# Two layers of gated recurrence and feed-forward on one core: first batch in channel halves, paired reciprocals, sums on GpSimd, idle-time products on TensorE, and a new order

## The chip, the core and the metric

The kernel runs on one core of a Trainium2 chip. The core's engines work side by side and wait for each other through semaphores: TensorE (PE, matmuls; PEld is its weight load), VectorE (DVE), ScalarE (ACT), GpSimd (POOL) and SyncE (SP, here only DMA issues). The metric is the device time of one execution in microseconds. All data is float32 but for two small bfloat16 masks.

## The reference

Four batches b of 256 tokens with 256 channels pass two layers l. Each layer has a conditioning part and a feed-forward part. The conditioning part is the same in both, with parameters w and u of its own (k and v are one input, `fside_BxSxS_0`; r is x):

```python
tf = sigmoid(sum(time_emb))
decay = exp(-exp(w)) * (0.5 + 0.5 * tf)
ek = exp(min(k, 30));  ekv = ek * v
# over tokens, forward and backward: a = a * decay + ekv ; b = b * decay + ek
num = nf + nb - ekv + exp(min(u + k, 30)) * v
den = df + db - ek + exp(min(u + k, 30))
out = sigmoid(r) * (num / max(den, 1e-8)) * (0.8 + 0.2 * tf)
```

Layer 0's feed-forward part adds to x a shared gated MLP (width 704) and eight routed experts (width 176, two per token, 320 slots each; a token's slot is its rank among the tokens of that expert in order). Layer 1's adds `relu(h @ W_up) @ W_down`, and `h @ W_expert` scaled by the weights of the two best of eight gates.

## The kernel before

**Tiles.** A tile n = 4 l + b is the conditioning part of one layer and batch, 128 partitions by 2 channel halves (c = 0, 1) by 256 tokens. `euk` (exp(u + k)) becomes the denominator and then its reciprocal; `euv` is euk * k and becomes the numerator; `df` and `nf` hold the scans of ek and ekv; `xc` holds x by channels and becomes h, the input of the feed-forward part.

**DVE** is the engine of the recurrence. `wkv(l, b, step)` has six steps: 0 forward scans of ek into df (L597, two, one per half); 1 forward scans of ekv into nf, and the cap on the next batch's ek (L609); 2 backward scans of df (L604), whose input `gd` ScalarE has scaled (L445); 3 euk + df (L639) and the floor at 1e-8 (L640); 4 backward scans of nf, and the cap on the next euk (L613); 5 two reciprocals (L647). For tiles 0 and 3 DVE then makes h too (L650, L653, L656); for tiles 1 and 2 GpSimd does (L343, L348, L351). In layer 1 step 5 ends with L660.

**The shared MLP** of a batch is six chunks c: TensorE multiplies h by up to 256 weight columns into one of three PSUM banks hb (`shared_up`), ScalarE takes the silu of one half (`silu`, L492), DVE multiplies by the other (`hidden`, L684). A bank is free when its chunk's `hidden` is done. `shared_down` closes a batch. `turn_rows` transposes h and makes the router's logits.

**Order.** Every engine's program is written out by tables indexed by the chunk c. `STEPS0` and `STEPS1` say how many steps of tiles 1 to 3 and 4 to 7 DVE does ahead of `hidden(c)`; `TURN_AT`, `RANK_AT`, `DOWN_BEHIND` place TensorE's transposes, ranks and down products; `ROUTE_AT` and `PLACE_AT` place DVE's routing of three rounds (batches 0 and 1; 2; 3); `SPREAD` places GpSimd's scatters of token rows to the experts' slots in DRAM (L355, two DMAs per 128 tokens). Tile 0's six steps come before everything else.

**After the last scatter** SP loads the slots (`buf`, L290, L291), TensorE transposes them and runs the eight experts (chunks 19 to 34), and DVE fits layer 1's tiles between. Then come batch 3's last shared chunks, 16 gathers of expert rows by GpSimd (L403; into the room of ek for batches 0 and 1 and of ekv for 2 and 3), and layer 1's feed-forward, batch after batch.

## Time and profile before

| | us |
|---|---|
| median of 3 runs (178.6 to 180.64) | 179.05 |
| the profiled execution's own time | 179.44 |
| its span, first to last instruction | 177.7 |
| PE busy, of the span | 144.6 |
| DVE busy | 134.6 |
| ACT busy | 71.2 |
| POOL busy | 69.2 |

A busy share is an average over stages with different limits, so the place of an idle stretch counts for more than its size. A timeline row gives start, length, engine, line, operation and tiles; "[x <-y]" is the engine's idle time just ahead of it and what ended it. One matmul of the program is two records of the trace.

### The profile page before, as it was taken

The page shows a single profiled execution, that of the slowest core. Times are in us where ns is not written, and L with a number is a line of the kernel's source. Part 1 is how long each engine was busy: PE and PEld are TensorE (multiplying, and loading weights), DVE is VectorE, ACT ScalarE, POOL GpSimd, SP SyncE. Part 2 cuts the span into 40 slices and gives each one's busy share as a digit, 9 for nine tenths or more (in the row PEclk, how much of TensorE's full clock was granted, in tenths as well). Part 3 has the DMA queues.
Part 4 walks back from the last instruction along what each step waited for, and adds up shares of the span by engine and source line. Part 5 has one row for each costly group of instructions (what it writes and reads, how often), then busy time and mean ns, then how long its engine had stood idle before and what let it go on. Part 6 is the DMA issues. An engine that isn't in the chain of part 4 may idle for free.

```text
span 177.7 us, 2207 instructions
## 1 busy us (share of the span) xinstructions
PE 144.6 (81%) x666; PEld 117.6 (66%) x666; DVE 134.6 (76%) x293; ACT 71.2 (40%) x168; POOL 69.2 (39%) x83
## 2 busy tenths in 40 slices
PE   0000297799999969995999999899999977999992
PEld 0000285688898858883777877677788856878781
DVE  0899979999998996724499969967589434787624
ACT  3699374454053005223427534623633201232330
POOL 5388022732487770560050050050002577762130
PEclk9999999789999999999999999999999999999998
DMA  4999999995002320129702072012104033332111
GB/s 96 255 340 369 395 413 258 194 279 200 1 31 96 111 87 32 37 48 331 281 1 74 3 221 74 30 44 76 61 17 148 30 116 90 112 101 89 59 59 59
DMA packets 14843, 23.61 MB, mean 133 GB/s; under 512 B 1974, under 2 KB 10375, under 8 KB 14704
## 3 DMA queue, kind: packets, MB, share of 16 engines
q1 hardware_dynamic: 13296, 19.49, 35.1%
q0 software_dynamic: 1536, 3.99, 7.1%
q8 instruction: 5, 0.08, 0.2%
q14 instruction: 6, 0.05, 0.1%
HBM read 15.29 MB, written 8.39 MB: 133 GB/s over the span
## 4 chain that ended last, share of the span: by engine, by line
PE 40%; DVE 33%; issue 9%; DMA 7%; POOL 7%; ACT 2%; SPq 0%; DVEq 0%; POOLq 0%; ACTq 0%
PE hb L833 23%; PE dn L833 10%; DVE euk L647 9%; POOL ek L403 4%; DVE df L604 4%; DVE nf L604 3%; PE tp L847 3%; DVE euk L639 2%; DMA buf<-slots_in 2%; DMA ekv<-slots_out,get_at 2%; DMA cond_s<-cond 2%; POOL ekv L403 2%; PE tp L923 2%; PE dk L833 2%; DVE df L597 1%
## 5 line engine op out<-in xcount | busy, mean ns | idle before, releaser
L833 PE MATMUL hb<-xc,sup_s 128*128 128x256 f32 x176 | 43.1, 404 | 2.3 <-DVE hid L684 2.3
L833 PEld LDWEIGHTS hb<-xc,sup_s 128*128 128x128 f32 x176 | 35.3, 204 | 8.2 <-DVE hid L684 3.1
L492 ACT ACTIVATE gate_a<-hb 128x256 f32<-128x256 f32 (+3 forms) x40 | 16.1, 403 | 35.5 <-PE hb L833 28.3
L343 POOL TENSOR_TENSOR euv<-euv,nf 128x512 f32<-128x512 f32 x6 | 7.8, 1296 | 55.6 <-DVE nf L604 55.6
L833 PE MATMUL hb<-bufT,mup_s 128*112 128x320 f32 (+1 forms) x96 | 27.3, 434 | 1.0 <-issue 0.5
L647 DVE RECIPROCAL euk<-euk 128x256 f32<-128x256 f32 x16 | 26.8, 1714 | 0.0
L847 PE MATMUL tp<-turn,xc 128*128 128x136 f32 x32 | 5.5, 325 | 22.4 <-DVE xc L656 22.4
L833 PEld LDWEIGHTS hb<-bufT,mup_s 128*112 128x112 f32 (+1 forms) x96 | 17.1, 181 | 9.1 <-issue 1.7
L833 PE MATMUL dn<-mdn_s,hidm 112*128 112x256 f32 x96 | 22.1, 380 | 0.0
L833 PE MATMUL dn<-sdn_s,hid 128*128 128x256 f32 x96 | 21.7, 381 | 0.1
L355 POOL DMA_INDIRECT slots_in<-htok,put_at x16 | 16.3, 1019 | 10.2 <-DVE put_at L729 5.8
L847 PEld LDWEIGHTS tp<-turn,xc 128*128 128x128 f32 x32 | 5.0, 225 | 22.9 <-issue 20.9
L833 PEld LDWEIGHTS dn<-sdn_s,hid 128*128 128x128 f32 x96 | 18.0, 190 | 2.8 <-DVE hid L684 0.5
L833 PEld LDWEIGHTS dn<-mdn_s,hidm 112*128 112x128 f32 x96 | 17.8, 190 | 2.7 <-issue 0.3
L684 DVE TENSOR_TENSOR hidm<-hb,gate_a 112x320 f32<-112x320 f32 (+1 forms) x16 | 7.6, 483 | 11.1 <-ACT gate_a L492 11.0
L684 DVE TENSOR_TENSOR hid<-hb,gate_a 128x256 f32<-128x256 f32 (+1 forms) x24 | 9.5, 412 | 4.6 <-ACT gate_a L492 4.5
L604 DVE TENSOR_TENSOR_SCAN df<-dk,df,gd 128x255 f32<-128x255 f32 x16 | 11.0, 724 | 0.9 <-ACT gd L445 0.9
L604 DVE TENSOR_TENSOR_SCAN nf<-dk,nf,gn 128x255 f32<-128x255 f32 x16 | 11.0, 731 | 0.1
L337 POOL TENSOR_TENSOR euv<-euk,k 128x512 f32<-128x512 f32 x8 | 10.2, 1274 | 0.4 <-DVE euk L613 0.4
L597 DVE TENSOR_TENSOR_SCAN df<-dk,ek 128x256 f32<-128x256 f32 x16 | 10.1, 668 | 0.0
L597 DVE TENSOR_TENSOR_SCAN nf<-dk,ekv 128x256 f32<-128x256 f32 x16 | 10.0, 661 | 0.0
L403 POOL DMA_INDIRECT ek<-slots_out,get_at x8 | 7.7, 956 | 5.6 <-DVE euk L660 3.5
(107 smaller groups left out, 203.1 us busy)
## 6 DMA issues: line engine op xcount, KB each, us to landing
mup_s<-mup SPq DMA_DIRECT2D x4, 704.0 KB, 15.3
slots_in<-outb SPq DMA_DIRECT2D x10, 256.0 KB, 9.2
slots_out<-outb SPq DMA_DIRECT2D x8, 256.0 KB, 2.2
...
```

Of the source, the lines that this page charges most:

```text
L337: nc.gpsimd.tensor_tensor(euv[:, n % 2], euk[:, l, b], k[:, b], ALU.mult).then_inc(euv_ready, 1)
L343: nc.gpsimd.tensor_tensor(euv[:, n % 2], euv[:, n % 2], nf[:], ALU.add).then_inc(num_ready[n], 1)
L355: nc.gpsimd.indirect_dma_start(out=slots_in, out_offset=bass.IndirectOffsetOnAxis(ap=put_at[:, j, n:n + 1], axis=0), in_=htok[:, n], in_of ...
L403: nc.gpsimd.indirect_dma_start(out=got_of(b, j, i), out_offset=None, in_=slots_out, in_offset=bass.IndirectOffsetOnAxis(ap=get_at[:, j, b ...
L492: nc.scalar.activation(dst, src, ACT.Silu).then_inc(silu_ready, 1)
L597: nc.vector.tensor_tensor_scan(fwd[:, c], d, src[:, b, c], 0.0, ALU.mult, ALU.add).then_inc(fwd_done, 1)
L604: nc.vector.tensor_tensor_scan(rev(both[:, c, 0:T - 1]), d, rev(gained[:, c, 0:T - 1]), both[:, c, T - 1:T], ALU.mult, ALU.add).then_inc(b ...
L639: after(tick(nc.vector.tensor_tensor(eu, eu, df[:], ALU.add)))
L647: nc.vector.reciprocal(eu[:, c], eu[:, c]).then_inc(den_ready, 1)
L684: nc.vector.tensor_tensor(dst, up, g, ALU.mult).then_inc(hid_ready, 1)
L833: return nc.tensor.matmul(dst, w, m, start=first, stop=last)
L847: last = nc.tensor.matmul(tp[i][:, at:at + P + E], xc[:, b, c, i * P:(i + 1) * P], turn[:, c], start=c == 0, stop=c == CH - 1, skip_group_ ...
```

## The change

- **First batch in halves.** Tile 0 is done by `first_tile` on DVE and `first_half` on GpSimd: both backward scans, the floor, the reciprocal and the product for half 0, then the same for half 1. `first_products` on TensorE does the transposes and the first four chunks (AHEAD) for half 0 when that half of h is there, and accumulates half 1 onto it. Those four chunks use three hb banks and one dn bank.
- **Paired reciprocals.** Tiles 1 to 7 form `pair` = d0 * d1 of the two halves, one reciprocal of 256 columns, and `rden` = pair times the denominators with halves exchanged.
- **Sums on GpSimd.** euk + df (`denominator`), the floor (for tiles not in MAX_ON_VECTOR), the numerator, and numerator times gated x run on GpSimd. The product with rden stays on DVE but for tile 1.
- **Idle-time products.** `idle_products` multiplies ident by k into a dn bank that nobody reads: 8 after the second forward scan of tile 0, 14 ahead of the transposes of batch 1.
- **Small ones.** The load of wu_s is issued by ScalarE; tf comes from a tanh; the router one-hots take fewer instructions; the output scale of layer 1 moves from L660 into ScalarE's relu and the mixing weights; the silu table is loaded by a dummy call; the gathers of batches 0 and 1 go into `buf` and wait for the stores and the transposes, not for the last tile; the memsets of padding move behind batch 1's work.
- **New order.** All tables have new numbers.

```diff
-TURN_AT = (6, 9, 14)
-ROUTE_AT = (6, 9, 14)
-RANK_AT = (8, 11, 15)
-PLACE_AT = (7, 10, 14)
-FETCH_AT = 23
+EARLY_AT = 2
+EARLY = 8
+FILL = {3: 14}
+AHEAD = 4
+
+TURN_AT = (3, 10, 15)
+ROUTE_AT = (3, 10, 15)
+RANK_AT = (6, 11, 15)
+PLACE_AT = (4, 12, 15)
+FETCH_AT = 28
...
-STEPS0 = (6, 0, 0, 3, 1, 0, 1, 1, 0, 2, 2, 1, 1, 0, 0, 0, 0, 0, 0)
-STEPS1 = (0, 0, 0, 0, 0, 0, 0, 0, 0, 0, 0, 0, 0, 0, 1, 0, 0, 2, 0, 1, 1, 1, 0, 3, 0, 2, 1, 4, 1, 0, 0, 1, 0, 2, 0)
-DOWN_BEHIND = (8, 13, 18)
-TAKE_BEHIND = (10, 16, 17)
-GATE_AT = (0, 5)
-SPREAD = {0: 1, 1: 4, 10: 5, 11: 5, 14: 5, 15: 8}
-H0_ON_VECTOR = (0, 3)
+STEPS0 = (4, 4, 0, 1, 0, 1, 1, 0, 1, 1, 1, 2, 0, 2, 0, 0, 0, 0, 0)
+STEPS1 = (0, 0, 0, 0, 0, 0, 0, 0, 0, 0, 0, 0, 0, 0, 0, 0, 0, 0, 5, 0, 0, 2, 2, 0, 0, 3, 0, 0, 1, 3, 0, 2, 0, 2, 0)
+DOWN_BEHIND = (7, 13, 17)
+TAKE_BEHIND = (13, 16, 18)
+GATE_AT = (3, 10)
+SPREAD = {7: 0, 9: 2, 10: 3, 14: 6, 15: 8}
+H0_ON_VECTOR = (0, 2, 3)
+Q1_ON_VECTOR = (0, 1, 2, 3)
+PADS_AT = (5, 5, 5, 5, 5, 5)
+MAX_ON_VECTOR = (1, 3, 4)
...
-        got = ek[:].rearrange("p b c t -> p (b c t)").rearrange("p (k n d) -> p k n d", k=2, n=TB * 2)
+        got = buf[:].rearrange("p q r d -> p (q r) d")[:, 0:8].rearrange("p (k n) d -> p k n d", k=2)
...
-        for kind, _, j in chunks:
+        for u, (kind, _, j) in enumerate(chunks):
             n = 2 if kind == "expert" and j == 0 else 1
+            if u < AHEAD:
+                chunk_banks.append([u])
+                continue
             chunk_banks.append([(unit + i) % 3 for i in range(n)])
             unit += n
...
-            sp.dma_start(wu_s[:], wu).then_inc(ld_small, 16)
...
+            def first_half(c):
+                pool.wait_ge(euv_ready, 1)
+                pool.wait_ge(bwd_done, 2 * c + 1)
+                nc.gpsimd.tensor_tensor(euk[:, 0, 0, c], euk[:, 0, 0, c], df[:, c], ALU.add).then_inc(den_summed, 1)
+                pool.wait_ge(bwd_done, 2 * c + 2)
+                nc.gpsimd.tensor_tensor(euv[:, 0, c], euv[:, 0, c], nf[:, c], ALU.add).then_inc(num_ready[0], 1)
+                pool.wait_ge(num_ready[0], c + 1)
+                pool.wait_ge(gate_ready, 1)
+                nc.gpsimd.tensor_tensor(euv[:, 0, c], euv[:, 0, c], xc[:, 0, c], ALU.mult).then_inc(gated, 1)
+
+            def denominator(l, b):
+                n = l * B + b
+                pool.wait_ge(euv_ready, n + 1)
+                pool.wait_ge(bwd_done, 4 * n + CH)
+                nc.gpsimd.tensor_tensor(euk[:, l, b], euk[:, l, b], df[:], ALU.add).then_inc(den_summed, 1)
+                if n not in MAX_ON_VECTOR:
+                    pool.wait_ge(den_summed, tiles_done(n))
+                    nc.gpsimd.tensor_scalar(euk[:, l, b], euk[:, l, b], 1e-8, None, ALU.max).then_inc(den_floored, 1)
+
             def numerator(l, b):
                 n = l * B + b
-                pool.wait_ge(euv_ready, n + 1)
                 pool.wait_ge(bwd_done, 4 * (n + 1))
                 nc.gpsimd.tensor_tensor(euv[:, n % 2], euv[:, n % 2], nf[:], ALU.add).then_inc(num_ready[n], 1)
 
-            def gate_h0(b):
+            def gate_num(b):
                 pool.wait_ge(num_ready[b], 1)
-                pool.wait_ge(den_ready, CH * (b + 1))
-                nc.gpsimd.tensor_tensor(euv[:, b % 2], euv[:, b % 2], euk[:, 0, b], ALU.mult).then_inc(q0_ready[b], 1)
-                pool.wait_ge(q0_ready[b], 1)
                 pool.wait_ge(gate_ready, b + 1)
-                nc.gpsimd.tensor_tensor(xc[:, b], xc[:, b], euv[:, b % 2], ALU.mult).then_inc(h0_ready[b], 1)
+                nc.gpsimd.tensor_tensor(euv[:, b % 2], euv[:, b % 2], xc[:, b], ALU.mult).then_inc(gated, 1)
+
+            def hidden0(b):
+                pool.wait_ge(gated, tiles_done(b))
+                pool.wait_ge(rden_ready, tiles_done(b))
+                nc.gpsimd.tensor_tensor(xc[:, b], euv[:, b % 2], rden[:], ALU.mult).then_inc(h0_ready[b], 1)
+
+            def base1(b):
...
-                    gate_h0(b)
+                    gate_num(b)
+                    if b not in H0_ON_VECTOR:
+                        hidden0(b)
...
-            pool.wait_ge(q1_ready, B)
+            pool.wait_ge(btp_ready, 3 * (E // 2))
             pool.wait_ge(routed, 1)
             for b in range(B):
+                if b == 2:
+                    pool.wait_ge(q1_ready, B)
...
+            act.dma_start(wu_s[:], wu).then_inc(ld_small, 16)
...
+                exp_uk0(b)
+                if b + 1 < B:
+                    exp_k(b + 1)
             for b in range(B):
-                exp_uk(1, b)
-            gate_x(1)
+                exp_uk1(b)
...
                     tanh_x1(b + 1)
...
                 if step == 0:
-                    if n == 0:
-                        cap_ek(0)
-                    v.wait_ge(ek_capped, b + 1)
+                    v.wait_ge(ek_ready[b], 1)
+                    v.wait_ge(den_summed, tiles_done(n - 1))
...
-                    v.wait_ge(bwd_done, 4 * n + CH)
-                    v.wait_ge(capped, n + 1)
-                    v.wait_ge(euv_ready, n + 1)
-                    after(tick(nc.vector.tensor_tensor(eu, eu, df[:], ALU.add)))
+                    backward(nf, gn, l, b, 4 * n + CH + 1)
+                    if n + 1 < B:
+                        cap_euk0(n + 1)
+                    if B <= n + 1 < 2 * B:
+                        cap_euk1(n + 1 - B)
+                elif step == 4:
+                    if n in MAX_ON_VECTOR:
+                        v.wait_ge(den_summed, tiles_done(n))
+                        after(tick(nc.vector.tensor_scalar(eu, eu, 1e-8, None, ALU.max)))
+                    else:
+                        v.wait_ge(den_floored, len([m for m in range(1, n + 1) if m not in MAX_ON_VECTOR]))
+                    after(tick(nc.vector.tensor_tensor(pair[:], eu[:, 0], eu[:, 1], ALU.mult)))
+                    after(tick(nc.vector.reciprocal(pair[:], pair[:])))
+                else:
+                    if 1 <= n <= B and n - 1 not in H0_ON_VECTOR:
+                        v.wait_ge(h0_ready[n - 1], 1)
+                    if n > B and n - 1 - B not in Q1_ON_VECTOR:
+                        v.wait_ge(q1_ready, n - B)
+                    nc.vector.tensor_tensor(rden[:], pair[:].unsqueeze(1).to_broadcast([P, CH, T]), eu[:, ::-1], ALU.mult).then_inc(rden_ready, 1)
+                    if l == 0 and b in H0_ON_VECTOR:
+                        v.wait_ge(rden_ready, tiles_done(n))
+                        v.wait_ge(gated, tiles_done(b))
+                        nc.vector.tensor_tensor(xc[:, b], euv[:, b % 2], rden[:], ALU.mult).then_inc(h0_ready[b], 1)
+                        v.wait_ge(h0_ready[b], 1)
...
+            def first_tile():
+
+                cap_ek(0)
+                v.wait_ge(ek_ready[0], 1)
+                forward(ek, df, 0, 0)
+                cap_euk0(0)
+                v.wait_ge(ekv_ready, 1)
+                forward(ekv, nf, 0, 0)
+                for c in range(CH):
+                    for both, gained, at in ((df, gd, 0), (nf, gn, CH)):
+                        v.wait_ge(scaled, at + c + 1)
+                        d = decay[:, 0, 0, c:c + 1].to_broadcast([P, T - 1])
+                        nc.vector.tensor_tensor_scan(rev(both[:, c, 0:T - 1]), d, rev(gained[:, c, 0:T - 1]), both[:, c, T - 1:T],
+                                                     ALU.mult, ALU.add).then_inc(bwd_done, 1)
+                    eu = euk[:, 0, 0, c]
+                    if c == 1:
+                        cap_ek(1)
+                    v.wait_ge(den_summed, c + 1)
                     after(tick(nc.vector.tensor_scalar(eu, eu, 1e-8, None, ALU.max)))
...
+                    nc.vector.reciprocal(rden[:, c], eu).then_inc(rden_ready, 1)
+                    if c == 1:
+                        cap_euk0(1)
+                    v.wait_ge(rden_ready, c + 1)
+                    v.wait_ge(gated, c + 1)
+                    nc.vector.tensor_tensor(xc[:, 0, c], euv[:, 0, c], rden[:, c], ALU.mult).then_inc(h0_ready[0], 1)
+                v.wait_ge(h0_ready[0], CH)
...
+            def first_products():
+
+                for c in range(CH):
+                    pe.wait_ge(h0_ready[0], c + 1)
+                    for i in range(TB):
+                        at = c * P
+                        last = nc.tensor.matmul(tp[i][:, at:at + P + E], xc[:, 0, c, i * P:(i + 1) * P], turn[:, c],
+                                                start=c == 0, stop=c == CH - 1, skip_group_check=True)
+                    if c == CH - 1:
+                        last.then_inc(htp_ready, 1)
+                    for u in range(AHEAD):
+                        if c == 0:
+                            pe.wait_ge(ld_sup[u // 2], 16)
+                        for half in range(2):
+                            at = u * CH * 2 * P + c * 2 * P + half * P
+                            last = nc.tensor.matmul(ub[u][:, half * T:half * T + T], sup_s[:, at:at + P], xc[:, 0, c],
+                                                    start=c == 0 and half == 0, stop=c == CH - 1, skip_group_check=True)
+                        if c == CH - 1:
+                            last.then_inc(up_ready, 1)
...
+            def idle_products(n):
+
+                for _ in range(n):
+                    mm(dn[1][:, 0:T], ident[:], k[:, 0, 0], True, True)
...
+            pe.wait_ge(fwd_done, EARLY_AT)
+            idle_products(EARLY)
+            first_products()
             for u in range(nearly):
+                if u < DOWN_BEHIND[1]:
+                    idle_products(FILL.get(u, 0))
                 if u in TURN_AT:
                     turn_rows(1 + TURN_AT.index(u))
-                shared_up(u)
```

**VectorE, tile 0 from the backward scans to h.** Before:

```order
L604 SCALAR_TENSOR_TENSOR df<-dk,df,gd 128x255 x2
L639 TENSOR_TENSOR euk<-euk,df 128x512
L640 TENSOR_SCALAR euk<-euk 128x512
L604 SCALAR_TENSOR_TENSOR nf<-dk,nf,gn 128x255 x2
L613 TENSOR_SCALAR euk<-euk 128x512
L647 RECIPROCAL euk<-euk 128x256 x2
L650 TENSOR_TENSOR euv<-euv,nf 128x512
L653 TENSOR_TENSOR euv<-euv,euk 128x512
L656 TENSOR_TENSOR xc<-xc,euv 128x512
```

Changed:

```order
L767 SCALAR_TENSOR_TENSOR df<-dk,df,gd 128x255
L767 SCALAR_TENSOR_TENSOR nf<-dk,nf,gn 128x255
L773 TENSOR_SCALAR euk<-euk 128x256
L774 RECIPROCAL rden<-euk 128x256
L779 TENSOR_TENSOR xc<-euv,rden 128x256
L767 SCALAR_TENSOR_TENSOR df<-dk,df,gd 128x255
L767 SCALAR_TENSOR_TENSOR nf<-dk,nf,gn 128x255
L702 TENSOR_SCALAR ek<-ek 128x512
L773 TENSOR_SCALAR euk<-euk 128x256
L774 RECIPROCAL rden<-euk 128x256
L706 TENSOR_SCALAR euk<-euk 128x512
L779 TENSOR_TENSOR xc<-euv,rden 128x256
```

The first product of h (xc) now comes after one half's work; the sums have left the engine.

**TensorE, from its first product to the transposes of batch 1.** Before:

```order
L847 MATMUL tp<-turn,xc 128x136 x4
L833 MATMUL hb<-xc,sup_s 128x256 x22
L847 MATMUL tp<-turn,xc 128x136 x4
```

Changed:

```order
L949 MATMUL dn<-k,ident 128x256 x8
L957 MATMUL tp<-turn,xc 128x136 x2
L966 MATMUL hb<-xc,sup_s 128x256 x6
L966 MATMUL dn<-xc,sup_s 128x256 x2
L957 MATMUL tp<-turn,xc 128x136 x2
L966 MATMUL hb<-xc,sup_s 128x256 x6
L966 MATMUL dn<-xc,sup_s 128x256 x2
L949 MATMUL dn<-k,ident 128x256 x14
L988 MATMUL tp<-turn,xc 128x136 x4
L949 MATMUL hb<-xc,sup_s 128x256 x10
```

Batch 1's transposes stood behind six chunks of batch 0 and now stand behind four and 14 idle products; chunks 4 and 5 of batch 0 follow them.

**GpSimd, from the second batch's sums on.** Before (here euv<-euv,nf is the numerator, xc<-xc,euv makes h):

```order
L337 TENSOR_TENSOR euv<-euk,k 128x512
L328 TENSOR_TENSOR ekv<-ek,k 128x512
L343 TENSOR_TENSOR euv<-euv,nf 128x512
L348 TENSOR_TENSOR euv<-euv,euk 128x512
L351 TENSOR_TENSOR xc<-xc,euv 128x512
```

Changed:

```order
L351 TENSOR_TENSOR ekv<-ek,k 128x512
L363 TENSOR_TENSOR euv<-euk,k 128x512
L351 TENSOR_TENSOR ekv<-ek,k 128x512
L379 TENSOR_TENSOR euk<-euk,df 128x512
L387 TENSOR_TENSOR euv<-euv,nf 128x512
L392 TENSOR_TENSOR euv<-euv,xc 128x512
L397 TENSOR_TENSOR xc<-euv,rden 128x512
```

A tile's denominator now passes through GpSimd between two steps of VectorE, and the numerator is gated ahead of the division.

## Rows read from the trace of the kernel before

**Rows 1.** Page: busy tenths of the span in 40 equal slices.

```profile
PE   0000297799999969995999999899999977999992
DVE  0899979999998996724499969967589434787624
```

**Rows 2.** The chain that ended last: start us, us, what.

```profile
6.90 1.27 DVE df L597 x2
...
10.04 1.38 DVE df L604 x2
...
20.08 0.70 DVE xc L656
...
65.03 0.70 DVE xc L656
65.77 1.19 PE tp L847 x8
...
78.53 0.38 SPq L290
...
83.83 3.46 PE hb L833 x12
```

**Rows 3.** Timeline, start-up of SP and DVE.

```profile
1.26 0.42 SPq L256 DMA_DIRECT2D cond_s<-cond  x1
...
5.24 0.17 DVE L584 TENSOR_SCALAR gate_t<-gate_t 128x4 f32<-128x4 f32 x1 [0.27 <-ACT gate_t L419]
...
5.66 0.17 DVE L586 TENSOR_SCALAR halfp<-gate_t 128x4 f32<-128x4 f32 x1
```

**Rows 4.** Groups by line and form: count, busy us, mean ns, idle before and its releaser.

```profile
L647 DVE RECIPROCAL euk<-euk 128x256 f32<-128x256 f32 x16 | 26.8, 1714 | 0.0
L639 DVE TENSOR_TENSOR euk<-euk,df 128x512 f32<-128x512 f32 x8 | 5.5, 686 | 0.2
L410 POOL TENSOR_TENSOR xt<-nf,xt 128x256 f32<-128x256 f32 x4 | 3.1, 792 | 8.2 <-ACT nf L565 8.2
```

**Rows 5.** Timeline, DVE instructions beside GpSimd's, and two alone.

```profile
13.43 1.80 POOL L378 MEMSET mdn_s<- 48x2048 f32 x1
...
14.04 1.47 DVE L613 TENSOR_SCALAR euk<-euk 128x512 f32<-128x512 f32 x1
...
40.86 0.39 DVE L613 TENSOR_SCALAR euk<-euk 128x512 f32<-128x512 f32 x1
...
48.14 1.27 POOL L351 TENSOR_TENSOR xc<-xc,euv 128x512 f32<-128x512 f32 x1
48.20 1.23 DVE L729 TENSOR_TENSOR put_at<-slot,over 128x8 uint32<-128x8 f32 x1
...
71.43 0.16 DVE L729 TENSOR_TENSOR put_at<-slot,over 128x4 uint32<-128x4 f32 x1
```

**Rows 6.** Timeline of TensorE.

```profile
22.86 7.04 PE L833 MATMUL hb<-xc,sup_s 128*128 128x256 f32 x24
...
32.25 6.27 PE L833 MATMUL hb<-xc,sup_s 128*128 128x256 f32 x20 [2.35 <-DVE hid L684]
...
44.57 5.43 PE L833 MATMUL dn<-sdn_s,hid 128*128 128x256 f32 x24
```

**Rows 7.** Windows: busy of PE, PEld, DVE, ACT, POOL; granted clock; DMA.

```profile
34.00:35.00 1.00, 1.00 (x3) 0.75 (x3) 1.00 (x3) 0.85 (x3) 1.00 (x2) 0.50 1.19 207
```

**Rows 8.** Timeline around the gathers; then DMA issues: count, KB, us to landing.

```profile
135.67 0.48 SPq L250 DMA_DIRECT2D slots_out<-outb  x1
...
137.64 0.75 DVE L660 SCALAR_TENSOR_TENSOR euk<-euv,oscale,euk 128x512 f32<-128x512 f32 x1
...
139.28 1.01 POOL L403 DMA_INDIRECT ek<-slots_out,get_at  x1 [3.52 <-DVE euk L660]
...
147.47 0.74 PE L979 MATMUL tp<-ident,xt 128*128 128x128 f32 x4 [1.93 <-DVE xt L783]
...
slots_out<-outb SPq DMA_DIRECT2D x8, 64.0 KB, 2.0
```

More of the change, by code:

```diff
@@ L73, in adaln_ffn @@
         euv = sb("euv", [P, 2, CH, T])
+        pair = sb("pair", [P, T])
+        rden = sb("rden", [P, CH, T])
         htok = sb("htok", [P, NT, C])
@@ L80, in adaln_ffn @@
         oscale = sb("oscale", [P, B])
+        halfo = sb("halfo", [P, B])
+        spare = sb("spare", [P, B])
+        minus = sb("minus", [P, B])
         ew = sb("ew", [P, 2, 2, CH])
@@ L550, in _ @@
             tanh_x1(0)
+            act.wait_ge(halfo_ready, 1)
             for b in range(B):
@@ L664, in hidden @@
             def hidden(c):
                 v.wait_ge(silu_ready, c + 1)
-                banks = [hb[i] for i in chunk_banks[c]]
+                banks = [ub[i] for i in chunk_banks[c]]
                 kind, b, j = chunks[c]
@@ L719, in place @@
                 v.wait_ge(pos_ready, r + 1)
[L720 to L723 removed]
+                n = (b1 - b0) * TB
+                counts = tp[0][:, s.start * E:s.stop * E].rearrange("p (n e) -> p n e", e=E).unsqueeze(1).to_broadcast([P, 2, n, E])
+                after(tick(nc.vector.tensor_tensor(ohp[:, :, s], counts, oh[:, :, s], ALU.mult)))
                 after(tick(nc.vector.tensor_reduce(pos[:, :, s], ohp[:, :, s], AX.X, ALU.add)))
[L725 removed]
+                tick(nc.vector.scalar_tensor_tensor(out=slot[:, :, s], in0=idx8[:, s, 0:2].rearrange("p n j -> p j n"), scalar=float(CAP), in1=pos[:, :, s],
                                                     op0=ALU.mult, op1=ALU.add))
@@ L741, in fetch @@
                 nc.vector.tensor_tensor(cw[:], cw[:], valid[:], ALU.mult).then_inc(routed, 1)
-            for step in range(STEPS):
-                wkv(0, 0, step)
+            first_tile()
             for c in range(nearly):
```

191 lines of the change are left out of this document (105 added, 86 removed).

## The prediction

> **What bounds the kernel now.** I read the page's slices first, then the chain in order of time, then the timelines around the places that it names. The slices [rows 1] show three parts: TensorE does nothing for the first tenth while DVE is full; then both are full up to slice 17; then TensorE alone is, to the end. The chain [rows 2] gives the hand-overs. DVE's scans begin at 6.90, h of batch 0 is done at 20.78 (20.08 + 0.70), h of batch 3 at 65.73, SP issues the slots' load at 78.53, the experts begin at 83.83. From there TensorE is fed by its own queue until the gathers. So a gain must come ahead of 78.53, or between the last expert and the first gathered row.
>
> **Start-up.** cond's load is issued second, at 1.26, and everything hangs on it; wu's issue ahead of it moves to ScalarE, so it starts some 0.45 earlier. Seven small DVE instructions become five: L584 to L586 took 0.42 for two [rows 3]. Scans start at 6.03, -0.87. ScalarE's own issue (0.4, as SP's) falls where ScalarE waits for cond; without that cover it would cost 0.4. The dummy silu moves a table load ahead of tile 1's scaling; ScalarE should be through near 19.8, when that scan ends, and each 1 us later would delay tile 1 by as much.
>
> **Tile 0.** Forward scans 1.27 and backward pairs 1.38 [rows 2] stay (pitches 1.2 and 1.4). Forward, a 0.35 cap and forward end at 8.75. Half 0: two backward scans 1.4 (10.15); GpSimd's half sum, 0.7 (L410 ran 0.79 with disturbance) [rows 4], then the floor 0.25, reciprocal 1.7 (1714 ns) [rows 4], product 0.4: 13.2 at the latest. Half 1: scans 1.4, cap 0.35, floor 0.25, reciprocal 1.65, cap 0.4, product 0.4, and waits behind GpSimd.
>
> Those waits are the unknown. In rows 5 a cap took 1.47 beside a memset, where the same one took 0.39 alone, and put_at took 1.23 and ended with L351, where it took 0.16 later [rows 5]. So a DVE instruction of these kinds waits out the GpSimd instruction that was first. GpSimd gets sums of 1.27 (L351's kind, [rows 5]), and they become ready when DVE's scan ends, just as DVE goes on to cap, floor and pair. Bounds: nothing, if they always miss each other; one whole 1.27 (0.7 in a half) for each of about six instructions a tile. I take a wait where my order of events has one: 0.75 and 0.95 in tile 0, 0.75 and 1.3 in tile 1, and 1 to 2 a tile after. h of batch 0 is then done at 18.6, -2.2; without waits at 16.9. The moved memsets (4.2 in a row now, behind batch 1's work) I count as one such wait, since a memset stood in the way of a cap in rows 5. The Trainium skill ("SBUF — State Buffer", Who interferes with whom) says that of the two whichever issues second is blocked for the other's whole length, which both pairs of rows bear out; and that an instruction with two SBUF inputs meets only a GpSimd one that reads, so a memset would hold up caps but not pairs. By that rule the sum would be up to 1.3 smaller where a pair meets the memsets; no row here has such a meeting.
>
> **Tile 1.** From 18.6: forward 2.4, cap 0.4, backward 2.6, cap 0.4, a hidden product 0.55, wait 0.75, floor 0.4, wait 1.3, pair 0.35 (half of L639's 686 ns) [rows 4], one reciprocal 1.7 where there were two, rden 0.7, and GpSimd's product 1.3: 31.4. Before, that h was done at 34.7. A tile costs DVE less by one reciprocal (1.7), L639 (0.7) and, for tile 3, two more products (1.3); it costs it more by pair and rden (1.05).
>
> **TensorE.** Before, three chunks (24 records) took 7.04 from a cold start, and 20 records 6.27 after an idle 2.35, where the clock was 0.50 [rows 6, 7]; 24 records of the down product took 5.43, 0.22 each. Now the 8 idle products run from about 7.5, cold at first, to 13; half 0's products, for whose weights the load is then just there, 14 to 18, half 1's to 22.7, 14 idle products (28 records at 0.22) to 28.9. Had they found no idle time they would cost 6.2; here they end before h of batch 1. They cost nothing and spare the two cold starts, 1.7 and 1.9, of which the first was already off the path now.
>
> From 31.4 to the transposes of batch 3, TensorE has nine full chunks (8 records, 1.76 each, 15.8), two short ones (1.8), two down products (5.3 each, 10.6), two times transposes (0.95, 1.9) and two ranks (0.5): 30.6, with no idle time, since all that it multiplies is there first. So the transposes of batch 3 begin at 62.0, before at 65.77 [rows 2]: **-3.8**. DVE in the same stretch: tile 2 with routing and placing 17, tile 3 with the same 13 to 14, from 30.1: h of batch 3 at 60.5 to 61. Both engines are within 1 us of each other, TensorE last.
>
> After the transposes one chunk, not two, stands before the ranks; but DVE's routing of about 1.1 and ScalarE's copies 1.2 now stand there too. I take 4.7 to the last put_at, where before it was 5.8 (65.77 to 71.59, [rows 2, 5]): **-1.1** more. Then four scatters, their landing and SP: 7.0 as before (71.59 to 78.53), if GpSimd is free: its six earlier scatters end near 64.4, 2 us before that would matter. TensorE's own queue ends near 74.5 and the first slots land near 76.3, so it isn't late. Slots' load and experts: -4.9.
>
> **Experts.** TensorE's work is the same 51; DVE has 1.7 less a tile. A burst of DVE steps (tile 5's last three, 5.1 plus one wait of 1.3) just fits between two experts' hidden products, some 6.2. No change.
>
> **Gathers.** They waited for L660 (end 138.39, start 139.28, so 0.9 from release to start). Now they wait for the last store: issued 135.67, landing 2.0 [rows 8], 137.7, start 138.6: **-0.7**. TensorE sat idle 1.93 there, so it takes it whole. ScalarE's mixing weights for batches 1 and 2 cost 0.4 more before GpSimd's sums; TensorE comes to those banks 1.4 or more later, so nothing.
>
> **Sum.** -3.8 - 1.1 - 0.7 = -5.6: 179.44, the profiled execution, becomes 173.8. That execution was 0.4 above the median of the three (179.05), so 173.4 for a median.
>
> **The rivals.**
> - *Cheap waits* (0.20). DVE and GpSimd rarely meet. h of batch 1 at 27.7; the idle products then are the last (28.9), so TensorE starts 2.5 earlier: 170.9. For it: rows 5 has as many undisturbed rows as disturbed ones. Against: sums start exactly at scan ends.
> - *The clock falls in front of batch 1* (0.15). If the gap between 28.9 and 31.4 does what 2.35 did at 32.25 [rows 6, 7], TensorE loses 1.9: 175.3. The Trainium skill ("TensorE: Matmul & The Clock Gate", What's actually happening) has the half rate as the idle state, which the 0.50 row agrees with. Against: a gap of 1.93 [rows 8] did no harm, and this one is 2.5 only if all waits come.
> - *DVE becomes the bound by waits, no gain* (0.14). At about 27 exposed instructions between 18.6 and 67, my waits average 0.2; at 0.4 h of batch 3 slips by 5.4 less 1 of slack: 177.8.
> - *Waits decide, slower* (0.08). Same place, but a mean of 0.55, near one half of a GpSimd sum each time: 14.9 - 5.4 - 1 = +8.5, 181.9. It decides from just over 0.5. For it: ten sums and products of 1.27 lay in the 51 us from h of batch 0 to the last put_at, a quarter of it; seventeen lie in 48 us now, 45%. Against: two or more waits a tile of full length would be needed, and a sum can't be ready that often.
> - *GpSimd becomes late for the scatters*: its floor on 512 columns is not in the trace; between a memset's 0.5 and twice a sum, 2.5. At 2.5 it costs nothing in layer 0, where it runs once ahead of tile 2's pair, but for 1.2 on DVE: inside the range.
>
> The forecast holds 0.43. Range: 170.6 to 178.0 leaves out the slower case and the ends of the others. What this kernel can tell from no change is about 1%, 1.8 us: under 177.3 is faster, over 180.8 slower. Faster: 0.43 + 0.20 + 0.15 and a part of the third, 0.79 less a little for what I have not seen: 0.78. Within 1%: 0.13. Slower: 0.09.
>
> **What would show it.** First scan near 6.0; first product of half 0 near 13.2 and of half 1 near 18.6; batch 1's transposes near 31.4, with the granted clock at 1 ahead of them; batch 3's near 62; last put_at near 66.7; slots' load near 73.5; TensorE without a gap from there to the last expert; first gather 0.9 behind the last store's landing. The waits are right if caps, floors and pairs of 0.4 appear as 0.8 to 1.6 beside GpSimd sums. Wrong would be: transposes of batch 3 behind h by DVE (DVE bound), experts starved by a DVE burst, or gathers still behind the last tile.

## The result and the profile after

The changed kernel takes 174.32 us (median of 4 runs, 173.31 to 176.63), against 179.71 for the kernel before in the same comparison: a ratio of 0.9677 [0.9626, 0.9728]. Faster, by 3.2%. Medians are over all executions of a kernel, ratios and their intervals over those in the chip's faster state alone. The profiled execution took 174.79, span 173.1, where the kernel before took 179.44: 4.65 less. The forecast was 5.6 less, 173.8 profiled and 173.4 for a median.

The page's slices of the changed kernel, for [rows 1] (each now 4.3 us):

```profile
PE   0399896899999999977999999999999979899991
...
DVE  0999999969879975999674953889678552695434
...
PEclk9999999699999999999999999999999999999999
```

TensorE has work from slice 1 on where it had none before slice 4. In the clock's row one digit is 6, at slice 7 (counted from 0, as the others), 30.3 to 34.6 us. The chain in order of time, for [rows 2]:

```profile
5.90 1.27 DVE df L686 x2
...
25.60 1.39 DVE pair L736
...
30.95 1.74 PE tp L988 x8
32.69 5.45 PE hb L949 x20
...
75.12 3.61 DMA buf<-slots_in
80.15 3.45 PE hb L949 x12
```

The same hand-overs in both kernels, and what was forecast:

| hand-over, us | before | forecast | after |
|---|---|---|---|
| first scan | 6.90 | 6.03 | 5.90 |
| h of batch 0 done | 20.78 | 18.6 | 18.32 |
| h of batch 1 done | 34.7 | 31.4 | 30.89 |
| transposes of batch 3 | 65.77 | 62.0 | 63.29 |
| last put_at | 71.59 | 66.7 | 67.78 |
| SP issues the slots' load | 78.53 | 73.6 | 74.70 |
| experts begin | 83.83 | 78.9 | 80.15 |
| first gather | 139.28 | 133.7 | 134.05 |

VectorE's timeline in tile 1, with GpSimd's beside it, answers to [rows 5]:

```profile
24.08 0.41 DVE L802 TENSOR_TENSOR hid<-hb,gate_a 128x256 f32<-128x256 f32 x1
24.41 1.16 DVE L733 TENSOR_SCALAR euk<-euk 128x512 f32<-128x512 f32 x1
25.60 1.37 DVE L736 TENSOR_TENSOR pair<-euk 128x256 f32<-128x256 f32 x1
27.01 1.75 DVE L737 RECIPROCAL pair<-pair 128x256 f32<-128x256 f32 x1
...
58.38 0.41 DVE L733 TENSOR_SCALAR euk<-euk 128x512 f32<-128x512 f32 x1
58.83 0.43 DVE L736 TENSOR_TENSOR pair<-euk 128x256 f32<-128x256 f32 x1
```

```profile
23.82 1.46 POOL L387 TENSOR_TENSOR euv<-euv,nf 128x512 f32<-128x512 f32 x1
25.36 1.33 POOL L392 TENSOR_TENSOR euv<-euv,xc 128x512 f32<-128x512 f32 x1
```

The floor is issued while GpSimd's numerator runs, and ends 0.3 behind it; the pair product is issued into GpSimd's gate product and ends 0.3 behind that. In tile 3 they took 0.41 and 0.43. There GpSimd's gate product ended 0.06 behind the floor's start, and only the issue of a scatter ran beside the pair:

```profile
57.17 1.27 POOL L392 TENSOR_TENSOR euv<-euv,xc 128x512 f32<-128x512 f32 x1
58.59 1.09 POOL L406 DMA_INDIRECT slots_in<-htok,put_at  x1 [0.15 <-DVE put_at L844]
```

TensorE's timeline around batch 1, for [rows 6, 7], and windows of 1 us (their length, five busy shares from PE to POOL, then the granted clock, ahead of DMA's share):

```profile
22.40 6.21 PE L949 MATMUL dn<-k,ident 128*128 128x256 f32 x28
30.95 1.74 PE L988 MATMUL tp<-turn,xc 128*128 128x136 f32 x8 [2.35 <-POOL xc L397]
```

```profile
30.00:31.00 1.00, 0.05 (x1) 0.05 (x1) 1.00 (x3) 0.80 (x2) 1.00 (x2) 1.00 1.16 295
31.00:32.00 1.00, 1.00 (x6) 1.00 (x7) 1.00 (x3) 0.85 (x3) 1.00 (x1) 0.72 1.07 194
32.00:33.00 1.00, 1.00 (x6) 0.91 (x5) 0.73 (x2) 1.00 (x4) 0.64 (x2) 0.50 1.14 219
33.00:34.00 1.00, 1.00 (x4) 0.82 (x3) 1.00 (x3) 1.00 (x6) 0.88 (x2) 0.50 1.09 237
34.00:35.00 1.00, 1.00 (x4) 0.79 (x4) 0.99 (x6) 0.97 (x2) 0.89 (x3) 0.57 1.16 247
35.00:36.00 1.00, 1.00 (x6) 0.90 (x5) 0.94 (x11) 0.47 (x3) 0.94 (x2) 1.00 0.97 201
```

The clock falls to 0.50, the 1.2 GHz level, behind the gap of 2.35, with TensorE fully busy in it. The end of the expert stretch:

```profile
130.35 1.48 DVE L736 TENSOR_TENSOR pair<-euk 128x256 f32<-128x256 f32 x1 [1.74 <-POOL euk L382]
...
131.28 0.48 SPq L274 DMA_DIRECT2D slots_out<-outb  x1
...
134.05 1.23 POOL L470 DMA_INDIRECT buf<-slots_out,get_at  x1 [2.49 <-issue]
```

The gathers follow the last store (131.28 plus its landing), while VectorE works on the last tile until 135.07.

### The profile page after: what moved, and what is told of

The parts are those of the page before. It is cut to its first block, busy times and chain, and to the rows that moved or that the text cites. A ratio compares the mean times of both kernels' runs of the same rounds, so it can differ in the third digit from the quotient of the medians.

```text
span 173.1 us, 2302 instructions
## 1 busy us (share of the span) xinstructions
PE 153.9 (89%) x710; PEld 125.2 (72%) x710; DVE 129.4 (75%) x272; ACT 74.3 (43%) x177; POOL 90.9 (52%) x101
## 4 chain that ended last, share of the span: by engine, by line
PE 56%; DVE 19%; issue 8%; DMA 7%; POOL 6%; ACT 2%; SPq 0%; DVEq 0%; POOLq 0%
PE hb L949 29%; PE dn L949 20%; POOL buf L470 4%; PE tp L1069 2%; DMA buf<-slots_in 2%; DVE nf L686 2%; PE dk L949 2%; DMA buf<-slots_out,get_at 2%; DVE df L686 2%; DMA wu_s<-wu 2%; PE tp L988 2%; DVE rden L774 1%; DMA slots_in<-htok,put_at 1%; DVE xt L892 1%; DVE pair L737 1%
## 5 line engine op out<-in xcount | busy, mean ns | idle before, releaser
L949 PE MATMUL hb<-xc,sup_s 128*128 128x256 f32 x144 | 34.3, 391 | 0.0
L949 PEld LDWEIGHTS hb<-xc,sup_s 128*128 128x128 f32 x144 | 27.8, 197 | 4.1 <-DVE hid L802 0.4
L379 POOL TENSOR_TENSOR euk<-euk,df 128x512 f32<-128x512 f32 x7 | 8.9, 1266 | 36.8 <-DVE df L693 36.5
L949 PE MATMUL dn<-k,ident 128*128 128x256 f32 x44 | 11.7, 430 | 7.3 <-DVE df L686 7.3
L949 PEld LDWEIGHTS dn<-k,ident 128*128 128x128 f32 x44 | 9.6, 220 | 8.9 <-issue 7.3
L517 ACT ACTIVATE gd<-df,gain 128x255 f32<-128x255 f32 x16 | 8.0, 506 | 13.1 <-DVE df L686 12.6
L737 DVE RECIPROCAL pair<-pair 128x256 f32<-128x256 f32 x7 | 12.3, 1753 | 0.2
L387 POOL TENSOR_TENSOR euv<-euv,nf 128x512 f32<-128x512 f32 x7 | 9.6, 1372 | 2.6 <-DVE nf L693 2.6
L736 DVE TENSOR_TENSOR pair<-euk 128x256 f32<-128x256 f32 x7 | 8.8, 1254 | 2.4 <-POOL euk L382 2.3
L470 POOL DMA_INDIRECT buf<-slots_out,get_at x8 | 7.9, 983 | 4.6 <-issue 4.6
```

Source lines behind the costliest of these rows:

```text
L379: nc.gpsimd.tensor_tensor(euk[:, l, b], euk[:, l, b], df[:], ALU.add).then_inc(den_summed, 1)
L387: nc.gpsimd.tensor_tensor(euv[:, n % 2], euv[:, n % 2], nf[:], ALU.add).then_inc(num_ready[n], 1)
L470: nc.gpsimd.indirect_dma_start(out=got_of(b, j, i), out_offset=None, in_=slots_out, in_offset=bass.IndirectOffsetOnAxis(ap=get_at[:, j, b ...
L517: nc.scalar.activation(dst[:, c, 0:T - 1], fwd[:, c, 0:T - 1], ACT.Copy, scale=gain[:, l, b, c:c + 1]).then_inc(scaled, 1)
L736: after(tick(nc.vector.tensor_tensor(pair[:], eu[:, 0], eu[:, 1], ALU.mult)))
L737: after(tick(nc.vector.reciprocal(pair[:], pair[:])))
```

## The experiments

Every kernel is the changed one with a small edit. Three comparisons were run; the kernel before had medians of 179.97, 180.34 and 180.05 in them, and each ratio is against its own.

| kernel | median us | ratio to before | gap before batch 1's transposes | batch 1's | batch 3's | between | clock there |
|---|---|---|---|---|---|---|---|
| the change | 174.32 | 0.9677 [0.9626, 0.9728] | 2.35 | 30.95 | 63.29 | 32.3 | fell |
| c0_changed | 174.85 | 0.9698 [0.9636, 0.976] | 2.33 | 30.94 | 63.29 | 32.4 | fell |
| e1_no_idle | 175.40 | 0.9681 [0.9626, 0.9736] | 7.86 | 30.83 | 64.40 | 33.6 | half from the start |
| e2_fill18 | 173.72 | 0.9682 [0.9629, 0.9736] | 0.61 | 31.24 | 62.35 | 31.1 | full |
| e3_early0 | 173.80 | 0.9689 [0.9634, 0.9744] | 1.85 | 30.87 | 61.98 | 31.1 | full |
| e4_unpaired | 173.67 | 0.9678 [0.962, 0.9736] | 1.82 | 30.40 | 61.39 | 31.0 | full |
| e5_gather_wait | 177.06 | 0.979 [0.9726, 0.9855] | 2.34 | 30.90 | 62.02 | 31.1 | full |
| e6_feed_whole | 179.56 | 0.9915 [0.987, 0.9959] | 2.85 | 34.75 | 67.04 | 32.3 | fell |
| e7_den_on_vector | 175.69 | 0.9755 [0.9691, 0.9818] | 3.01 | 31.83 | 64.16 | 32.3 | fell |
| e8_turned_later | 177.87 | 0.9827 [0.976, 0.9893] | 1.42 | 34.10 | 65.21 | 31.1 | full |
| e9_unpaired_fill18 | 173.50 | 0.9665 [0.961, 0.972] | 0.1 | 30.48 | 61.47 | 31.0 | full |
| e10_no_gpsimd_floor | 174.09 | 0.9668 [0.9623, 0.9712] | 2.34 | 30.90 | 63.06 | 32.2 | fell |
| e11_floor_on_vector | 173.16 | 0.9641 [0.9585, 0.9697] | 0.1 | 30.47 | 61.46 | 31.0 | full |

"Fell" is a granted clock of 0.50 for some 3 us behind those transposes. The distance in the seventh column is 31.0 to 31.1 in every profile at full clock and 32.2 to 32.4 in every one that fell. The medians are too close together to tell a loss of 1.2 between two kernels; this column isn't.

A second place decides too, and only some profiles meet it: in e1, e5, e6 and e8 the clock fell to 0.50 again at the start of the experts, between 77 and 88 us. So the ends of those profiles aren't compared with the others' as they stand. The rows from e5:

```profile
77.80 1.53 PE L1070 MATMUL tp<-ident,buf 128*128 128x128 f32 x6 [1.05 <-DMA buf<-slots_in]
```

```profile
78.00:79.00 1.00, 1.00 (x6) 0.92 (x5) 1.00 (x1) 0.06 (x1) 0.00 (x0) 0.50 0.96 299
```

The same six records took 0.88 in the changed kernel, behind a gap of 0.56.

**c0_changed**, unedited, beside the first edits.

> The changed kernel as it is, for comparison within this series. Both theories: 173.3 to 174.8, ratio to before 0.965 to 0.972. My theory of the clock: runs with a mean granted clock of 1.00 are near 173.5 and those at 0.99 near 174.8 or more, because only in the latter TensorE falls to 1.2 GHz after the 2.35 us gap in front of batch 1's transposes. Rival: the spread is of other origin and does not go with the clock.

174.85 and 0.9698; the fall of the clock came again. The theory of the clock holds: of the changed kernel's executions here and in the section before, the three with a mean granted clock of 1.00 have spans of 171.6 to 172.1, the four at 0.986 to 0.99 of 172.8 to 173.3, and the three at 0.98 of 174.2 to 174.9. The same kernel has both outcomes, about 1.2 apart.

**e1_no_idle.**

```diff
-EARLY = 8
-FILL = {3: 14}
+EARLY = 0
+FILL = {}
```

> Both groups of idle products are left out. Theory A (their only worth is the clock, and they lie off the path): TensorE starts batch 0's products cold, ends them near 24.5, is idle for 6 us and is cold again for batch 1: every run is as the changed kernel's slow-clock ones, about 174.8, +0.5 to +1.3 on its median. Rival B (cold first products hold up the first hidden product and so VectorE): +2.5 or more. Rival C (they cost more than they bring): 0 or less.

175.40, and 0.9681 is not to be told from the control's 0.9698. Half 0's products were slow (12 records of hb in 3.83, after idle products 2.86), although the profile's clock reads 1.00 there; half 1's ended at 22.98 instead of 22.56, and the gap grew to 7.86. Batch 1's h came at 30.8 all the same. In the profile the whole set of idle products is worth 1.1 at batch 3 (64.40 against 63.29): TensorE began at the half clock instead of falling to it. That excludes the rival of +2.5 or more; between the other two the medians don't decide. The early ones warm an engine ahead of work with slack; the 14 stop 2.3 us short of where they would save the rest.

**e2_fill18.**

```diff
-FILL = {3: 14}
+FILL = {3: 18}
```

> 18 idle products instead of 14 ahead of batch 1's transposes: they end near 30.4 instead of 28.6, still before h of batch 1 (30.9), and the gap is 0.5 instead of 2.35. Theory (the gap lets the clock fall in some runs): granted clock 1.00 in every run, 173.2, -0.3 to -1.2 on the median of the changed kernel. Rival (the clock falls for another reason, or costs nothing on the path): no change.

173.72, profiled span 171.8. Five of the six executions kept a mean clock of 0.999 or 1.00, one had 0.99 (175.66), so not "every run". TensorE in the profile, then its windows:

```profile
31.24 1.19 PE L988 MATMUL tp<-turn,xc 128*128 128x136 f32 x8 [0.61 <-POOL xc L397]
```

```profile
32.00:33.00 1.00, 1.00 (x8) 0.92 (x7) 0.73 (x3) 0.92 (x4) 0.64 (x2) 1.00 1.12 140
33.00:34.00 1.00, 1.00 (x7) 0.87 (x5) 1.00 (x3) 1.00 (x6) 1.00 (x1) 1.00 1.12 150
```

No fall. Locally the fall costs 1.7 (transposes 1.74 and 20 records of hb 5.66 in the changed kernel, 1.19 and 4.48 here); at full speed TensorE waits for VectorE's hidden product behind them (0.33 at 37.17), so 1.2 to 1.3 reach batch 3. Batch 1's h came 0.3 later than in the changed kernel's profile, but the added products didn't do that: everything is 0.3 later here from the first idle product on (7.61 for 7.32). They end 0.6 short of h.

**e3_early0** takes away the 8 early products alone.

```diff
-EARLY = 8
+EARLY = 0
```

> The 8 idle products ahead of batch 0 are left out, the 14 ahead of batch 1 stay. Theory A (clock and gap): half 0's products run cold from 13.3 to about 20, half 1's to 24, the 14 end near 30, so the gap in front of batch 1 closes by itself and nothing on the path is late: 173.3, the changed kernel's time with a full clock. Rival B: the first hidden product (24.1) is late by the cold start and VectorE waits: +0.5 to +1.5.

173.80, and the slow start (half 0's 12 records of hb took 3.80, from 14.40) cost nothing at batch 1: 30.87. TensorE ended its 14 products later, at 29.03, so its gap was 1.85 and the clock held. Taking away a warm-up shortened the gap that mattered.

**e4_unpaired** takes two reciprocals straight from the denominators.

```diff
-after(tick(nc.vector.tensor_tensor(pair[:], eu[:, 0], eu[:, 1], ALU.mult)))
-after(tick(nc.vector.reciprocal(pair[:], pair[:])))
-...
-nc.vector.tensor_tensor(rden[:], pair[:]..., eu[:, ::-1], ALU.mult)
+nc.vector.reciprocal(rden[:, 0], eu[:, 0])
+nc.vector.reciprocal(rden[:, 1], eu[:, 1]).then_inc(rden_ready, 1)
```

> Tiles 1 to 7 take two reciprocals of 256 columns straight from the denominators again, without pair and without the product that makes rden; all else as changed. Theory A (undisturbed prices: pair 0.4 and rden 0.7 for a reciprocal of 1.71): +0.65 a tile on VectorE, h of batch 1 0.65 later, +0.6 to +1.5 in all. Theory B (the wait for GpSimd's port: pair took 1.25 on average in the changed kernel, a reciprocal does not wait): pair and rden 1.95 against 1.71, so h of batch 1 0.25 to 0.9 earlier and the time -0.2 to -0.9. Rival C: the wait moves to the product behind it, no change.

173.67, span 170.9. Groups of VectorE by line, e4 and then the changed kernel:

```profile
L738 DVE RECIPROCAL rden<-euk 128x256 f32<-128x256 f32 x7 | 12.3, 1751 | 3.5 <-POOL euk L382 3.4
L739 DVE RECIPROCAL rden<-euk 128x256 f32<-128x256 f32 x7 | 11.9, 1693 | 0.0
```

```profile
L737 DVE RECIPROCAL pair<-pair 128x256 f32<-128x256 f32 x7 | 12.3, 1753 | 0.2
...
L736 DVE TENSOR_TENSOR pair<-euk 128x256 f32<-128x256 f32 x7 | 8.8, 1254 | 2.4 <-POOL euk L382 2.3
...
L743 DVE TENSOR_TENSOR rden<-pair,euk 128x512 f32<-128x512 f32 x7 | 4.8, 687 | 0.2
```

The pairing replaced a reciprocal of 1.69 by a product that averages 1.25, since GpSimd blocks it, and one of 0.69: 1.94. It saves nothing; undisturbed (0.43 + 0.69) it would save 0.57. Without it h of batch 1 is 0.55 earlier, in part given back later, where VectorE now waits 3.5 instead of 2.4 for GpSimd's floor. A reciprocal lasts 1.68 to 1.75 beside GpSimd's operations or not. Three of the six executions had a clock of 1.00 and spans of 170.9 to 171.2; the others, at 0.99, 172.7 or more. So even this kernel loses the clock at times; the profile doesn't show where.

**e5_gather_wait** gives GpSimd the wait for the last tile back.

```diff
             pool.wait_ge(btp_ready, 3 * (E // 2))
+            pool.wait_ge(q1_ready, B)
```

> All gathers wait for the last tile of layer 1 again, though those of batches 0 and 1 still go into buf. Theory (the release of the gathers counts whole): the last tile's product ended 135.07 in the changed kernel, so the first gather starts at 135.95 instead of 134.05, +1.9, of which TensorE takes at least 1.5: +1.5 to +1.9. Rival (the tail has slack behind the gathers): under +0.5.

177.06, 2.2 above the control's median and 1.7 by the ratios, and in the profile the last tile lets the gathers go:

```profile
136.27 1.06 POOL L471 DMA_INDIRECT buf<-slots_out,get_at  x1 [4.44 <-DVE euk L753]
```

In the control that row stands at 133.91, 2.4 earlier. Of these, 0.4 are not the edit's: the last store was issued at 131.54 for 131.13, because the slots landed 0.4 later behind their issue and the clock fell at 78 us. The wait itself costs 1.9 to 2.0, what was expected. The prediction priced it at 0.7, from the distance that it had in the old schedule. In the new one the last tile is later against the experts: GpSimd's sum and its floor (1.26 + 1.48) and a pair product of 1.48 stand in front of its reciprocal.

This kernel had the same gap before batch 1 as e10 and kept its clock there. First e5, then e10:

```profile
30.90 1.20 PE L989 MATMUL tp<-turn,xc 128*128 128x136 f32 x8 [2.34 <-POOL xc L397]
```

```profile
30.90 2.18 PE L988 MATMUL tp<-turn,xc 128*128 128x136 f32 x8 [2.34 <-POOL xc L397]
```

**e6_feed_whole** lets TensorE wait for both halves of batch 0.

```diff
-                    pe.wait_ge(h0_ready[0], c + 1)
+                    pe.wait_ge(h0_ready[0], CH)
-FILL = {3: 14}
+FILL = {3: 8}
```

> TensorE takes batch 0 only when both halves of h are there, and has 8 instead of 14 idle products behind it, so that they end near 30 again. VectorE and GpSimd still work by halves. Theory A (TensorE's early half is off the path, since it has idle products to spare): the first chunk is ready at 21.5 to 23, the first hidden product waits up to 0.5, 0 to +0.5 in all. Rival B (the head start of TensorE is where the gain of the halves comes from): +2 or more.

179.56; by the ratio 0.9 of the gain's 3.0% are left. That TensorE's head start lies off the path was wrong. VectorE's timeline:

```profile
20.95 1.38 DVE L693 TENSOR_TENSOR_SCAN df<-dk,df,gd 128x255 f32<-128x255 f32 x2
26.25 1.39 DVE L693 TENSOR_TENSOR_SCAN nf<-dk,nf,gn 128x255 f32<-128x255 f32 x2 [3.92 <-ACT gn L517]
```

ScalarE executes in order, and its copies of batch 0's transposes stand between the scales gd and gn of tile 1. TensorE, at half clock from 16 to 22 us after a gap of 4.89, finished those transposes near 25, so gn, and with it h of batch 1, came 3.8 later. The gap of 2.85 ahead of it brought the clock down as well.

**e8_turned_later** is e6 with those copies behind gn.

```diff
-            turned(0)
             if STEPS0[0] >= 2:
                 scale_fwd(0, 1, 1)
+            turned(0)
```

> As e6_feed_whole (TensorE waits for both halves of h of batch 0, 8 idle products), but ScalarE's two gn scales of tile 1 are issued ahead of its copies of batch 0's transposes (the htok and lg copies). Theory A (what e6 lost is ScalarE's queue: gn of tile 1 stood behind transposes that a cold TensorE finished 6 us later): gn of tile 1 runs by 21, h of batch 1 is back at 31 to 32 instead of 34.7, and the median is 174.5 to 176. Theory B (the loss was TensorE's own late start of about 5 us): h of batch 1 may come early but the time stays at 178.5 to 179.6. The feeding by halves alone is then worth what is left between this run and the changed kernel: A says 0 to 1.2.

177.87, between the two ranges. gn ran at 20.14 and the scans no longer waited, as the first theory has it, but h of batch 1 came only 0.65 earlier (34.10 for 34.75); the other 1.2 at batch 3 is the clock, which held. A second wait had taken the first one's place:

```profile
23.49 0.53 DVE L706 TENSOR_SCALAR euk<-euk 128x512 f32<-128x512 f32 x1
28.27 0.42 DVE L802 TENSOR_TENSOR hid<-hb,gate_a 128x256 f32<-128x256 f32 x1 [4.25 <-ACT gate_a L563]
28.62 1.05 DVE L733 TENSOR_SCALAR euk<-euk 128x512 f32<-128x512 f32 x1
```

VectorE's queue has the hidden product of chunk 0 ahead of tile 1's floor, and that product needs TensorE's first chunk through the silu. Both theories missed this. Without the feeding by halves, h of batch 1 comes 3.2 later (34.10 against 30.94), the median is 3.0 higher and the ratio 0.0129, 2.3 us, because TensorE's first results stand in VectorE's path twice: over ScalarE's queue, and by way of this product.

These 3.2 are not the price of the later feeding alone. The gap of 5.77 ahead of batch 0 had brought the clock down:

```profile
19.34 5.11 PE L966 MATMUL hb<-xc,sup_s 128*128 128x256 f32 x12
```

```profile
20.00:21.00 1.00, 1.00 (x3) 0.78 (x3) 1.00 (x4) 0.85 (x3) 0.00 (x0) 0.50 1.05 404
```

Half 0's records took 7.05 (18.27 to 25.32) for 4.32 in the changed kernel (13.32 to 17.64). By an estimate from these rows some 2.7 of the 4.25 that VectorE waited are the clock's. No run fed both halves at once with TensorE kept at full clock, so how much the halves are worth by themselves stays open.

**e7_den_on_vector** puts sums and floors of tiles 1 to 7 back on VectorE, and its sum into the step of the backward scan:

```diff
+                    v.wait_ge(bwd_done, 4 * n + CH)
+                    nc.vector.tensor_tensor(eu, eu, df[:], ALU.add).then_inc(den_summed, 1)
-MAX_ON_VECTOR = (1, 3, 4)
+MAX_ON_VECTOR = tuple(range(1, 8))
```

> Tiles 1 to 7 have the sum euk + df and the floor on VectorE again (0.69 and 0.43 alone); GpSimd keeps the numerators and their gating. Theory A (VectorE's instructions count on the path to batch 1, waits stay as they are): h of batch 1 0.7 later, +0.7 to +1.8 in all. Theory B (GpSimd's load makes VectorE's waits, 1.0 a tile): the waits shrink by as much as the sums add, -0.3 to +0.4.

175.69, batch 1's transposes 0.9 later, of which 0.2 were there at the first scan (6.12 for 5.90); the gap 3.0 and the clock down. The pair product still lasted 1.37 in the median: the operation that blocks it is GpSimd's numerator or gate product, not the sum. So sums and floors on GpSimd gain about 0.7 at batch 1 in the profile, and 0.8 in the medians, whose intervals overlap.

**e9_unpaired_fill18** is e4 with e2.

> The changed kernel with both edits that looked good apart: two reciprocals straight from the denominators (no pair product, no re-multiplication) and 18 idle products in place of 14. Theory A (the two act at different places, VectorE's path to h of batch 1 and TensorE's clock in front of it): no slice of TensorE at the lower clock at 31 to 35, h of batch 1 at 30.3, span 170.5 to 171.3, median 172.2 to 173.2, about 1.5 below the changed kernel. Rival B (each only takes away the same 1.9 us of half clock, so together they give no more than one): 173.5 to 173.9 median.

173.50, in the rival's range. Batch 3's transposes came no earlier than in e4 (61.47, 61.39): at a gap of 1.82 e4's profile had not lost the clock either. There both edits remove the same loss.

**e10_no_gpsimd_floor.**

```diff
-                if n not in MAX_ON_VECTOR:
+                if False:
...
-                        v.wait_ge(den_floored, ...)
+                        v.wait_ge(den_summed, tiles_done(n))
```

> The changed kernel without the floor of 1e-8 that GpSimd lays under the denominators of tiles 2, 5, 6 and 7 (part of the computation is left out there; four instructions of about 1.5 us). Theory A (GpSimd's floor holds VectorE twice, as releaser of the pair product and as its neighbour on the port): the idle time in front of the pair product falls from 2.4 to below 0.8 and its mean from 1.25 to about 1.0; h of batch 2 comes up to 1.5 earlier, but TensorE has the work in hand there and the experts are TensorE's, so the time moves by 0 to -1.0: 173.8 to 174.8. Rival B (VectorE with its waits is the bound behind batch 1): each 1.5 us is felt in the end, 171.5 to 173.

174.09, inside the first theory's range. Its group line:

```profile
L736 DVE TENSOR_TENSOR pair<-euk 128x256 f32<-128x256 f32 x7 | 8.0, 1140 | 0.3 <-POOL euk L379 0.2
```

The idle time fell from 2.4 to 0.3, the mean only from 1254 to 1140 where 1000 was expected: without the floor GpSimd's next operation meets the pair instead.

**e11_floor_on_vector** is e9 with all floors of tiles 1 to 7 on VectorE (MAX_ON_VECTOR = 1 to 7).

> e9 with all floors of tiles 1 to 7 on VectorE (0.43 us undisturbed each, up to 1.5 beside a GpSimd operation) in place of GpSimd's of about 1.5 us; the sums stay on GpSimd. Theory A (two-input work of GpSimd is what holds VectorE; a floor on VectorE is cheaper in the stretch before the experts and free in the expert stretch): equal to e9 or up to 0.7 faster, 171.7 to 173.0. Rival B (each floor on VectorE is caught beside the numerator or gate product of GpSimd and lasts 1.2 to 1.5 itself): 0 to 1 slower than e9, 172.5 to 174.

173.16, the lowest median of all: 0.3 below e9, but outside the first theory's range (to 173.0) and inside the rival's. The rival's mechanism is in the trace: VectorE's floors take 1.16 in the median and up to 1.49. It is not slower for that. Its interval overlaps with e9's and the changed kernel's (0.9641 [0.9585, 0.9697] against 0.9677 [0.9626, 0.9728]); at a clock of 0.996 or more its four spans of 170.7 to 171.2 lie below the changed kernel's 171.6 to 172.1, taken in other comparisons. That it beats the change by some 1 us is likely, not shown. It has fewer products and no idle gap.

## Why the prediction was right

**Start-up**: first scan 5.90 for 6.03. Right in size, but with less cover than told: wu on ScalarE's queue landed 3.19 behind its issue, and gate_t ran at 4.35 only 0.11 behind the exponentials that need wu.

```profile
0.79 0.40 ACTq L481 DMA_DIRECT2D wu_s<-wu  x1
...
4.00 0.20 ACT L483 ACTIVATE ew<-wu_s 128x4 f32<-128x4 f32 x1 [1.50 <-DMA wu_s<-wu]
4.24 0.20 ACT L485 ACTIVATE ew<-ew 128x4 f32<-128x4 f32 x1
4.35 0.19 ACT L487 ACTIVATE gate_t<-zsum 128x4 f32<-128x4 f32 x1
```

**Waits between VectorE and GpSimd**: the unknown of the forecast, and well sized. Taken were 0.75 and 1.3 for tile 1's floor and pair; they took 0.75 and 0.94 over their undisturbed 0.41 and 0.43. Over the stretch from 18.3 to 67 the rows that stand above their undisturbed length add up to 4.7 (0.16 + 0.75 + 0.94 + 0.27 + 0.72 in caps, floor and pairs, 0.37 + 0.41 + 1.05 in placing), against 5.4 taken. VectorE waited for no result of GpSimd in that stretch: its two waits for GpSimd's floor, 2.3 together, come in layer 1. By that, neither *cheap waits* nor the two rivals of costly waits came about. The placing row of 1.05 is the kind that [rows 5] had shown. The wait that was counted for the moved memsets didn't come: they ran from 33.88 to 37.94 beside scans and routing of the usual lengths, and no cap or pair met them.

**Tile 1 and TensorE**: h of batch 1 at 30.89 for 31.4. From there to batch 3's transposes 30.6 of work was counted; 31.0 is what undisturbed profiles need. What failed in part is the sentence that the idle products "spare the two cold starts": the second one, behind batch 0, was not spared. The gap was 2.35 and the clock fell, the mechanism of the rival *the clock falls in front of batch 1*, to which 0.15 had been given. It cost 1.3 at batch 3, not 1.9, and turns the 62.0 into 63.29: -0.45 from h, +0.4 work, +1.3 clock. Three other executions of this kernel had a mean clock of 1.00, so no such fall; they took 173.31 to 173.85, where the forecast of 173.4 lies. The argument against that rival, that a gap of 1.93 did no harm, was true and did not reach to 2.35. The Trainium skill ("TensorE: Matmul & The Clock Gate", What's actually happening) has the half rate as the idle state; the windows above agree on the level, but show the fall behind the gap, in work. In the longer gaps of e1, e6 and e8 it fell while TensorE stood idle (e1: 0.50 from 27 us, in the gap of 7.86).

**To the slots' load**: transposes to last put_at 4.5 for 4.7, put_at to SP 6.9 for 7.0 (67.78 to 74.70). Right.

**Experts**: forecast no change; 50.13 (80.15 to 130.28) after 50.85 (83.83 to 134.68). The 0.7 came unforeseen. The timelines place nearly all of it: in the kernel before TensorE stood waiting for one hidden product of VectorE, and from 106.81 to the row below it took 7.33, where the like stretch takes 6.70 now (103.10 to 109.80) without a wait.

```profile
114.14 3.46 PE L833 MATMUL hb<-bufT,mup_s 128*112 128x320 f32 x12 [0.46 <-DVE hidm L684]
```

**Gathers**: 133.7 was forecast, 134.05 measured. The term of 0.7 was right: the experts ended 4.4 earlier and the gathers began 5.2 earlier, 0.8 more. That isn't what the edit is worth in the new schedule. By e5 it is 1.9 to 2.0 there, since the last tile slipped behind the experts (it ended 3.7 behind their last product before, 4.8 now). Behind the first gather 0.6 of the 5.2 was given back: the end moved by 4.6 (span 177.7 to 173.1), as the rows of batch 1 landed 3.45 behind their last issue, where 2.8 is the median of the gathers. That cause is read from the chain alone.

**The halves** were told as the way to an earlier first product. e6 and e8 show more: without the step 3 us are lost at batch 1, partly through the clock, since TensorE's results return into VectorE's queue ahead of tile 1's floor. The forecast had this order right in its times and did not name the dependence.

**Not tested**: the new order of the tables was never run without the rest, nor the rest without it, so what it brings by itself (1.3 between batch 3's transposes and the last put_at, in the table above) is read from the rows alone.
